# First stage of an AdaLN, attention and int8 product kernel: other load order, weights transposed into the score banks, demodulation in two parts

## What is computed

```
x = x * s1;  x = (x - mean) * rsqrt(var + 1e-5)
dc(W, s) = rsqrt(einsum('oi,bi->bo', W**2, s**2) + 1e-8)
q = heads(x @ q_weight.T * dc(q_weight, s1));  k = heads(x @ k_weight.T * dc(k_weight, s1))
v = x @ v_weight.T * dc(v_weight, s1) * s2
attn = softmax(q k^T / sqrt(16)) ;  out = (attn v) @ w_weight.T * dc(w_weight, s2)
out += (v @ u_weight.T) * dc(u_weight, s2)
result = x + int8_product(out, rhs)      # row scales of out, column scales of rhs
```

## Time and profile before

| what | us |
|---|---|
| three runs, median (lowest to highest) | 460.46 (459.71 to 461.0) |
| the profiled execution, its own time | 460.14 |
| its span, first to last instruction of the program | 458.1 |
| TensorE busy in the span | 419.1 (91%) |
| ScalarE busy | 291.8 (64%) |
| VectorE busy | 245.4 (54%) |
| GpSimd busy | 100.7 (22%) |
| first score matmul starts at | 46.59 |

### The profile page before, as it was taken

One profiled execution on the slowest core, in us unless ns is written; L12 is line 12 of the kernel. 1 busy time (PEld: TensorE's weight loads), 2 busy tenths in 40 slices (PEclk: granted clock), 3 DMA queues, 4 the chain that ended last, 5 costly groups with the idle time before them and its releaser, 6 DMA issues.

```text
span 458.1 us, 7640 instructions
## 1 busy us (share of the span) xinstructions
PE 419.1 (91%) x2626; PEld 232.0 (51%) x2626; DVE 245.4 (54%) x564; ACT 291.8 (64%) x333; POOL 100.7 (22%) x116
## 2 busy tenths in 40 slices
PE   5882899999998999999999999899999999999873
PEld 4771454455554555555545555455544555554341
DVE  3764346454466546744675447654674445436144
ACT  3120578767777686668765787568676776578731
POOL 4241311301212023301250024202340123002112
PEclk9997699999999999999999999999999999999997
DMA  7059239903993199515992299418931399202021
GB/s 228 14 131 198 49 111 129 128 11 100 129 127 66 36 158 127 101 51 148 126 140 54 91 136 128 107 39 157 152 76 54 74 122 131 79 2 93 0 92 47
DMA packets 29790, 45.15 MB, mean 99 GB/s; under 512 B 3928, under 2 KB 15448, under 8 KB 29704
## 3 DMA queue, kind: packets, MB, share of 16 engines
q1 hardware_dynamic: 27840, 40.02, 52.0%
q0 software_dynamic: 1072, 3.74, 2.5%
q10 hardware_dynamic: 832, 0.80, 0.6%
HBM read 15.09 MB, written 4.28 MB: 42 GB/s over the span
## 4 chain that ended last, share of the span: by engine, by line
PE 79%; DVE 9%; SPq 4%; issue 3%; DMA 2%; ACT 2%; POOL 0%; POOLq 0%; ACTq 0%; DVEq 0%
PE o_acc L901 23%; PE scores L887 16%; PE work L944 11%; PE work L864 9%; PE work L923 9%; PE work L1015 6%; SPq L261 3%; PE work L932 3%; PE work L1161 2%; PE work L1029 2%; ACT probs L473 1%; DMA x_res<-in_L_cond_w_weight_dram 1%; DVE o_t L672 1%; DVE amax L668 1%; DVE o_t L665 1%
## 5 line engine op out<-in xcount | busy, mean ns | idle before, releaser
L473 ACT ACTIVATE probs<-scores 128x1024 f32<-128x1024 f32 x256 | 247.6, 1024 | 105.5 <-PE scores L887 105.5
L901 PE MATMUL o_acc<-probs,v_aug 128*32 128x512 f32 x1024 | 123.1, 598 | 0.0
L887 PE MATMUL scores<-q_stack,k_stack 50*128 50x512 f32 x512 | 96.5, 451 | 14.1 <-SPq L270 7.4
L887 PEld LDWEIGHTS scores<-q_stack,k_stack 50*128 50x128 f32 x512 | 39.6, 186 | 87.2 <-ACT probs L473 60.6
L397 POOL TENSOR_TENSOR squares<-parts 128x512 bf16<-128x512 f32 x32 | 33.3, 1040 | 217.3 <-ACT parts L463 217.3
L901 PEld LDWEIGHTS o_acc<-probs,v_aug 128*32 128x32 f32 x1024 | 26.7, 109 | 60.9 <-issue 56.0
L944 PE MATMUL work<-vs_w,x_t 128*128 128x512 f32 x192 | 53.8, 425 | 0.0
L923 PE MATMUL work<-x_t,qk_w 128*128 128x512 f32 x192 | 51.1, 409 | 0.6 <-DVEq L567 0.6
L944 PEld LDWEIGHTS work<-vs_w,x_t 128*128 128x128 f32 x192 | 36.1, 199 | 13.0 <-issue 5.9
L597 DVE TENSOR_TENSOR v_aug<-work,rows 128x256 f32<-128x256 f32 x32 | 13.6, 425 | 51.4 <-PE work L944 51.4
L923 PEld LDWEIGHTS work<-x_t,qk_w 128*128 128x128 f32 x192 | 34.8, 191 | 8.4 <-DVEq L567 1.0
(11 more groups left out here) (109 smaller groups left out, 376.1 us busy)
## 6 DMA issues: line engine op xcount, KB each, us to landing
q_stack<-parts SPq DMA_DIRECT2D x96, 128.0 KB, 5.6
k_stack<-parts SPq DMA_DIRECT2D x96, 128.0 KB, 7.7
x_sb<-in_x_dram SPq DMA_DIRECT2D x8, 512.0 KB, 3.6
x_res<-in_x_dram SPq DMA_DIRECT2D x8, 512.0 KB, 4.6
out_dram<-res POOLq DMA_DIRECT2D x7, 512.0 KB, 8.0
rows<-rows_dram SPq DMA_DIRECT2D x8, 384.0 KB, 3.4
rows<-in_cond_dram SPq DMA_DIRECT2D x8, 128.0 KB, 3.6
q_stack<-const_dram SPq DMA_DIRECT2D x16, 32.0 KB
```

The source lines that it names most:

```text
L473: nc.scalar.activation(probs[:, r % RING, pair:pair + 2, :], scores[:, pair:pair + 2, :], ACT.Exp).then_inc(exp_done, 1)
L887: last = nc.tensor.matmul(scores[:, 2 * (u % 2) + e, :], k_stack[top:top + ROWS, t % 2, 2 * g + u % 2, kt * P:(kt + 1) * P], q_stack[top:t ...
L901: last = nc.tensor.matmul(o_acc[DV * j:DV * (j + 1), :], v_aug[:, kt, 4 * g + j, :], probs[:, r % RING, j, :], start=(kt == 0), stop=(kt = ...
```

## The change

It touches the first stage and the places that depend on it.

- **Loads.** SP loads x of element 0 in two halves with the style row between them, then wu and rhs; ScalarE's queue loads the conditioning, wq, wk, wv, ww. wv is loaded once, into its natural place.
- **Weights.** TensorE transposes each weight into a score bank or o_acc (first_bank) instead of a work bank, wq and wk with the head order already in the destination pattern. ScalarE squares from there and writes the rounded part, or for ww and wu the plain copy; VectorE writes the rests. The copies by VectorE are gone.
- **Demodulation.** Query and key sums come first, right behind their transposes; their root, reciprocal and refinement are on ScalarE and VectorE. The other three weights follow, refined on GpSimd. ScalarE loads the tables of Sqrt and later of Exp by a small activation each.
- **TensorE filler.** keep_clock, matmuls of the ones with the identity whose results nobody reads: 8 before the conditioning, 8 before the x transposes; the 4 at L1175 are gone.
- **x transposes and fold of element 0.** ScalarE writes the rounded part, VectorE the rest.
- **Projections of element 0** go to the score banks in the order q0, k0, q1, k1, then fold.
- **Stack rows.** Instead of constant rows by DMA, GpSimd fills k_stack with ones, VectorE the first half of q_stack with zeros, GpSimd the second half of both after its squares of element 0. zero_shift is done from element 2 on.
- **Key stacks of element 0** are sent by ScalarE's queue (12 DMAs, between its high parts), query stacks by SP (12 DMAs), with load_rows(0) between them.
- **x of element 1** is loaded behind load_shift(0).

The diff, cut to its core:

```diff
-    ORDER = ([("cond", 0, 0)] + [("weight", 0, m) for m in range(5)] + [("sums", 0, 0)]
-             + [("xt", 0, 0), ("xt", 0, 1), ("rows", 0, 0), ("rows", 0, 1)]
-             + [("q", 0, 0), ("k", 0, 0), ("q", 0, 1), ("fold", 0, 0), ("k", 0, 1), ("norms", 0, 0), ("v", 0, 0)])
+    ORDER = [("cond", 0, 0), ("sums", 0, 0), ("sums", 0, 1), ("xt", 0, 0), ("xt", 0, 1), ("rows", 0, 0), ("rows", 0, 1),
+             ("fold", 0, 0), ("norms", 0, 0), ("v", 0, 0)]
...
         @block.sync
-            for m, w in ((WQ, wq), (WV, wv), (WU, wu)):
-                sp.dma_start(w_nat[m], w.rearrange("(c p) i -> p c i", p=P)).then_inc(w_loaded[m], 16)
-            load_x(0)
-            sp.dma_start(wv_nat[:, :, :], wv.rearrange("(c p) i -> p c i", p=P)).then_inc(wv_loaded, 16)
-            sp.wait_ge(pool_stored, 16)
-            zero_shift(0)
-            sp.wait_ge(const_stored, 16)
-            for par in range(2):
-                for e in range(2):
-                    sp.dma_start(k_stack[e * HALF + BIAS:e * HALF + ROWS, par, :, :].bitcast(F32), const_dram[1]
-                                 ).then_inc(ones_loaded, 16)
+            first = x[0].rearrange("(k p) h -> p k h", p=P)
+            sp.dma_start(x_sb[:, 0:2, :], first[:, 0:2, :]).then_inc(first_x[0], 16)
+            sp.dma_start(rows[:, 0, :], cond[0, 0:H].partition_broadcast(P)).then_inc(style_loaded, 16)
+            sp.dma_start(x_sb[:, 2:4, :], first[:, 2:4, :]).then_inc(first_x[1], 16)
+            sp.dma_start(w_nat[WU], wu.rearrange("(c p) i -> p c i", p=P)).then_inc(w_loaded[WU], 16)
+            sp.dma_start(rhs_nat, rhs.rearrange("(c p) o -> p c o", p=P)).then_inc(rhs_loaded, 16)
             sp.wait_ge(demod_rows_ready, 1)
             sp.dma_start(rows_dram[:, :, :], demod_rows[:, :, :]).then_inc(rows_stored, 16)
-            sp.wait_ge(xt_ready, 2)
-            load_x(1)
+            sp.wait_ge(q_cleared[0], 1)
+            for part in range(2):
+                load_stack(0, 0, part)
             sp.wait_ge(rows_stored, 16)
             load_rows(0)
-            load_stacks(0)
+            for part in range(2):
+                load_stack(0, 2, part)
             load_shift(0)
+            load_x(1)
+            sp.wait_ge(q_cleared[1], 1)
+            sp.wait_ge(k_cleared, 2)
+            sp.wait_ge(zero_stored, 16)
...
         @block.gpsimd
-            for value in range(2):
-                nc.gpsimd.memset(const_rows[:, value, :], float(value)).then_inc(ones_ready, 1)
...
+            nc.gpsimd.memset(zero_rows, 0.0).then_inc(pool_setup, 1)
+            nc.gpsimd.memset(k_stack[:, 0, :, :].bitcast(F32), 1.0).then_inc(k_cleared, 1)
...
             for n in range(4):
                 square(0, n)
+            nc.gpsimd.memset(k_stack[:, 1, :, :].bitcast(F32), 1.0).then_inc(k_cleared, 1)
+            nc.gpsimd.memset(q_stack[:, 1, :, :].bitcast(F32), 0.0).then_inc(q_cleared[1], 1)
             inverse_root(1)
...
         @block.scalar
+            act.wait_ge(const_ready, 2)
+            nc.scalar.activation(table[:, :], ones[:, 0:1], ACT.Sqrt)
...
+            squared(WQ)
+            rounded(WQ, qk_w[:, 0, WQ, :, :], split_hi)
+            squared(WK)
+            rounded(WK, qk_w[:, 0, WK, :, :], split_hi)
+            roots(slice(0, 2 * HC), 1)
+            squared(WV)
+            squared(WW)
+            squared(WU)
+            rounded(WV, vs_w[:, 0, :, 0:H], split_hi)
+            rounded(WW, ww_t[:, :, :], ww_ready)
+            rounded(WU, wu_t[:, :, :], wu_ready)
+            roots(slice(2 * HC, 5 * HC), 2)
+            nc.scalar.activation(table[:, :], ones[:, 0:1], ACT.Exp)
+            for c in range(HC):
+                use = USE[("xt", 0, c)]
+                act.wait_ge(work_ready, use + 1)
+                nc.scalar.activation(x_t[:, 0, c, :], work[:, use % NW, :], ACT.Copy).then_inc(first_hi, 1)
...
+            high_part(0, 0)
+            high_part(0, 1)
+            act.wait_ge(k_cleared, 1)
+            load_first_keys(1, 0)
+            high_part(0, 2)
+            load_first_keys(1, 1)
+            high_part(0, 3)
+            load_first_keys(3, 0)
+            use = USE[("fold", 0, 0)]
+            act.wait_ge(work_ready, use + 1)
+            nc.scalar.activation(vs_w[:, 0, :, H:2 * H], work[:, use % NW, :].rearrange("p (c o) -> p c o", c=HC), ACT.Copy
+                                 ).then_inc(first_hi, 1)
+            load_first_keys(3, 1)
...
         @block.vector
+            nc.vector.memset(q_stack[:, 0, :, :].bitcast(F32), 0.0).then_inc(q_cleared[0], 1)
             link(nc.vector.memset(head_ones[:, :], 0.0))
...
+            for i in range(2):
+                two = slice(2 * i, 2 * i + 2)
+                dve.wait_ge(first_x[i], 16)
...
+            rest(WQ, qk_w[:, 0, WQ, :, :], qk_w[:, 1, WQ, :, :], 1)
+            sums(0, qk_chunks)
+            rest(WK, qk_w[:, 0, WK, :, :], qk_w[:, 1, WK, :, :], 2)
             normalise_x(0)
...
+            bank = ready("fold", 0, 0).rearrange("p (c o) -> p c o", c=HC)
+            dve.wait_ge(first_hi, HC + 1)
+            link(nc.vector.tensor_tensor(vs_w[:, 1, :, H:2 * H], bank, vs_w[:, 0, :, H:2 * H], ALU.subtract))
...
             largest_norms(0)
             bound_flag(0)
...
         @block.tensor
+            keep_clock(work[:, NW - 1, :], 8)
             pe.wait_ge(cond_loaded, 16)
...
+            transposed(WQ)
+            transposed(WK)
+            pe.wait_ge(cond_ready, 1)
+            bank = claim("sums", 0, 0)
+            summed(bank, WQ, 0)
+            summed(bank, WK, 1).then_inc(work_ready, 1)
+            transposed(WV)
+            transposed(WW)
+            transposed(WU)
+            bank = claim("sums", 0, 1)
+            summed(bank, WV, 0)
+            summed(bank, WW, 1)
+            summed(bank, WU, 2).then_inc(work_ready, 1)
+            keep_clock(claim("xt", 0, 0), 8)
             x_transposed(0, 0)
             x_transposed(0, 1)
...
-            for _ in range(4):
-                nc.tensor.matmul(scores[:, 0, 0:P], ones[:, :], ident[:, :], start=True, stop=True)
             projected("q", 0, 0)
             projected("k", 0, 0)
             projected("q", 0, 1)
+            projected("k", 0, 1)
             skip_matrix(0)
-            projected("k", 0, 1)
```

More of the change, by code:

```diff
@@ L316, in _ @@
                         load_x(a + 1)
-                    load_stacks(a)
+                    for n in range(4):
+                        for part in range(2):
+                            load_stack(a, n, part)
                     load_shift(a)
@@ L571, in low_part @@
                 g = n // 2
[L572 removed]
+                bank = scores[:, n, :] if a == 0 else ready("k" if n % 2 else "q", a, g)
                 dve.wait_ge(hi_ready, a * 4 + (n + 1))
@@ new lines, in sums @@
+            def sums(i, chunks):
+                n = chunks.stop - chunks.start
+                link(nc.vector.tensor_scalar(demod_sum[:, chunks, :],
+                                             ready("sums", 0, i)[:, 0:n * B].rearrange("p (c b) -> p c b", b=B),
+                                             EPS_DEMOD, None, ALU.add))
+                dve.sem_inc(work_freed, 1)
+                dve.sem_inc(demod_summed, 1)
+            qk_chunks, other_chunks = slice(0, 2 * HC), slice(2 * HC, 5 * HC)
@@ new lines, in _ @@
+            dve.wait_ge(style_loaded, 16)
+            for i in range(2):
+                two = slice(2 * i, 2 * i + 2)
+                dve.wait_ge(first_x[i], 16)
+                link(nc.vector.tensor_tensor(x_sb[:, two, :], x_sb[:, two, :],
+                                             rows[:, 0, :].unsqueeze(1).broadcast_to([P, 2, H]), ALU.mult))
+                for k in (2 * i, 2 * i + 1):
+                    last = nc.vector.bn_stats(stats[:, k, :], x_sb[:, k, :])
+            link(last)
@@ new lines, in _ @@
+            for k in range(KT):
+                last = nc.vector.bn_aggr(mv[:, k, :], stats[:, k, :])
+            link(last)
+            nc.vector.tensor_scalar(var_eps[:, :], mv[:, :, 1], EPS_NORM, None, ALU.add).then_inc(var_ready, 1)
+            rest(WQ, qk_w[:, 0, WQ, :, :], qk_w[:, 1, WQ, :, :], 1)
+            sums(0, qk_chunks)
+            rest(WK, qk_w[:, 0, WK, :, :], qk_w[:, 1, WK, :, :], 2)
+            normalise_x(0)
+            root, square = demod[:, qk_chunks, :], demod_t[:, qk_chunks, :]
@@ new lines, in _ @@
+            sums(1, other_chunks)
+            rest(WV, vs_w[:, 0, :, 0:H], vs_w[:, 1, :, 0:H], 3)
+            dve.wait_ge(root_ready, 2)
+            nc.vector.reciprocal(demod[:, other_chunks, :], demod[:, other_chunks, :]).then_inc(inverse_ready, 1)
+            for c in range(HC):
+                bank = ready("xt", 0, c)
+                dve.wait_ge(first_hi, c + 1)
+                link(nc.vector.tensor_tensor(x_t[:, 1, c, :], bank, x_t[:, 0, c, :], ALU.subtract))
+                dve.sem_inc(work_freed, 1)
+                dve.sem_inc(xt_ready, 1)
@@ L915, in projected @@
```

(12 more changed lines are left out.)

241 lines of the change are left out of this document (119 added, 122 removed).

## The result

| | before | after |
|---|---|---|
| median of four runs each (lowest to highest), us | 460.37 (459.71 to 461.0) | 471.96 (471.56 to 472.4) |
| ratio after to before, 95% interval | | 1.0256 (1.0231 to 1.0282) |
| span of the profiled execution, us | 458.1 | 469.7 |
| first projection starts at | 25.21 | 28.29 |
| first scores start at | 46.59 | 47.69 |

The changed kernel is 11.6 us slower; 456.5 had been forecast, with a range up to 461.0. Both the sign and the range were missed. Ratios leave out executions in the chip's slower state, of which there is one in this document (the run of 469.62 us). The page shows the loss in two places: a wait of output matmuls for VectorE's last write of the skip path, and key stacks that need 12.5 us to land.

A forecast was written before the change was run, and what follows sets the result against it. The start was taken as bounded by TensorE's sums, VectorE's serial work and SP's issue time. First projection 23.2 plus 29.0 put the second output matmuls at 52.2 against 56.15: 460.46 - 4.0 = 456.5 us, range 452.6 to 461.0.

The forecast's parts named there:

- x(1) lands in 4.2 us: Load of x of element 1, issued behind the flag: 4.2 us from issue to landing, ends 3.5 and 8.3.
- First projection at 23.2: TensorE's first projection of element 0 starts at 23.2 us instead of 25.21; bounds 19.8 (fast clock throughout) and 25.7 (slow).
- doesn't lift it: Rival: the first keep_clock doesn't raise TensorE's clock; first projection at 25.7, 1.4 us gained, 459.1 us; chance 0.20.
- From the projection to the flag +15.2: ScalarE's queue with 12 key DMAs as the chain: flag 15.2 us after the first projection, before +12.3.
- First scores at +17.3: TensorE's first scores start 17.3 us after the first projection, at 40.5 instead of 46.59, following the value projection.
- Modulation to normalisation 7.05: VectorE's work on x of element 1, from modulation to normalisation, takes 7.05 us, as before the change.
- the point: Reference instant, start of TensorE's second group of output matmuls: forecast at 52.2 us against 56.15 before.
- The stages after are a pattern that only shifts: Everything after the second group of output matmuls (56.15 us before) keeps its pattern and shifts by whatever that instant shifts.
- Slower: x(1) is late: Rival: VectorE's modulation of x(1) delays values 1 to 3; landing 8.3, point at 58.8, 463 us; chance 0.09.
- The clear of q_stack blocks GpSimd: Rival: VectorE's clear holds up GpSimd's ident and ones; keep_clock starts near 6, 4.3 us later; 460.8 us; chance 0.07.
- ScalarE's tables: No extra table loads taken around the first root; otherwise up to 2.6 us more, 1 us of it in the range.
- The 4 us forecast as a gain: Second group of output matmuls 4.0 us earlier, 52.2 against 56.15, taken off the whole time.

## Why the prediction was wrong, by its steps

- **x(1) lands in 4.2 us, "nearest to the undisturbed load": this step failed.** 12.9 were measured, 8.7 us more. Both its ends, 3.5 and 8.3, were landings of other loads (8.3 that of x of element 0, 3.5 those of later elements), with other traffic ahead; x(1) itself had landed in 5.7 us before, ahead of the stacks. The step left out what stands ahead in the DMA engines. The resource was in the rows and not read: the share of 1.02 in 36 to 38. By the forecast's own times 3.54 MB, from +3 on at 205 GB/s (the mean of five 4-us windows before, from 28 on), end at +20; at the issue at +16.4 about 0.8 MB would be left, and with 0.65 of its own that is 7 us. So 3 of the 8.7 us could have been read ahead at that rate; the other 6 came from the lower rate after. That low rates occur was to be seen as well, in the next stage of the kernel before (128 GB/s from 70 to 90, at a share of 1.08); with it the same sum gives 19 us. By these two rates the range for this term was 7 to 19 us, an estimate.
- **First projection at 23.2:** 28.29, above the upper bound of 25.7. Q's weights, with x ahead of them, let TensorE start at 8.30, where the forecast had it start at 5.6 and put a wait for them at nothing; it was 2.27 us. The first keep_clock bought nothing, the second step that failed: the forecast had the first 24 of the 40 sums at the fast pace, but it was followed by that wait, and all 40 together took 8.55 us (3.42 and 5.13), at the pace of the earlier trace rows. The rival "doesn't lift it" had this, without the wait.
- **From the projection to the flag +15.2:** +15.6. ScalarE's queue as the chain, with the fold's rounding behind its issues, was as described (the 12 issues took 0.66 us each, 0.64 had been taken), and the kernel that rounds ahead of six issues shows it by taking most of that wait away. First scores at +17.3: +19.4, by a wait of 2.1 us for a key stack, again the full DMA engines.
- **Modulation to normalisation 7.05:** 7.03. With q at +28.29, flag +15.64, issue 1.29 and 0.44, landing 12.9, 7.03 and 0.67 the point is at 66.2; 14.1 us over the forecast of 52.2, of which 8.7 are the landing, 5.1 the first projection, 0.3 the rest.
- **The stages after are a pattern that only shifts:** not quite. The wait was long enough for TensorE's clock to fall, which cost 3 us more.
- **Slower: x(1) is late (0.09):** the right mechanism, in the right place, with the wait at the values of element 0. Its price (463) came from the same 8.3 us. A landing of which no row showed the size needed a wider bound and more than 0.09.
- **The clear of q_stack blocks GpSimd** fell: the clear took 3.47 us, GpSimd's of k_stack 3.51 at the same time, and GpSimd's ones ended at 1.66 as before. GpSimd's later clear of the same size, from 38.16, took 3.51 too, most of it while VectorE stood idle. The rows that it went by show only VectorE's step slowed (2.50 against 1.38); "the two hinder each other" was more than they say. The rival had drawn on the exclusive lock in the Trainium skill (SBUF — State Buffer) without its narrower rule in "Who interferes with whom": a VectorE instruction with at most one SBUF input, outside the two-port modes, doesn't contend with GpSimd. A clear has no input, and the trace agrees with that. **ScalarE's tables** were as taken: two loads in the first stage, at 3.97 and 22.40, both asked for, and none between squares and roots. The Trainium skill (ScalarE: Activation LUTs, "Table sets: the hidden batching unit") names copy among the cheap functions that are in every set, and the trace agrees; it doesn't name the square there, for which only the trace shows it.
- **The 4 us forecast as a gain** don't come with this change and x(1) early (1.002). With Q's weights first as well the gain is 2.6 us, without the fillers 3.2, and 5.0 with the filler in a wait and the fold ahead of six issues. The first of these takes back a wait that the forecast had left out; the other two take away costs that were in its sum.
- **A slip in a sum:** with the first projection at 19.8 the same terms give 7.35 us of gain and not 7.2. Nothing hangs on it.

## What to carry to other kernels

A load that is moved in the issue order is priced by the bytes that stand ahead of it in the DMA engines and their rate, and not by its landing time in a quiet stage or by the sender's pace. Four kernels bear the count out (12.9 against 13, 8.0 against 8.5, 9.6 against 9.8, 12.1 against 10.8), but with rates read afterwards: ahead of time the rate is a range. Look at the DMA share of the windows first, and ask which engine's next instruction waits for the last in line. A second sender added less than the intervals tell when that share was at 1. Filler matmuls on the path cost 3.8 us here and gave back 1.5; four calls in a wait gave the projections their 5.86 us back, without a gain in the medians that is clear of the noise.

## What was unexpected of the hardware

- The same 24 DMAs of 131 KB moved at 123 to 173 GB/s in the changed kernel and at 204 to 258 with x(1) early, at the same DMA share; a kernel that differs from the latter only by a filler moved them at 133 to 196, and the kernel before moves those of its next stage at 128. No run here shows why.
- 8-column sums do run at the pace of the high clock when it is granted: 16 in 1.94 us against 3.42, and 24 in 2.96 in the kernel with x(1) behind six stacks against 5.13. Which of the two paces the 24 had differed between kernels with the same instructions up to there. It may be part of the scatter of one kernel (459.26 to 463.13 us for the one with x(1) early); no run shows that.
- A wait of 8.5 us of TensorE cost 3 us beyond itself, by the granted clock of 0.5 from 62.5 to 72.8.
